# Layer 0's context in three parts, and other orders at the start of four stages, in a four-layer transformer kernel

## The reference

```
x = x + xattn_L(layernorm(x), ctx);  x = x + ffn_L(layernorm(x))        L = 0..3
L0 xattn: x1 = LN(q_in)*g1+b1; x2 = LN(ctx)*g2+b2; k = x2@Wk+bk; v = x2@Wv+bv
          softmax(q k^T / 16) v @ Wo + bo          (one head of 256, per batch)
L0 ffn:   8-way router, top 2; silu(x@w0.T+b0)*c0 + silu(x@w1.T+b1)*c1
L1 xattn: 8 heads of 128 over all tokens and all context rows
L1 ffn:   rows rounded to 8 bits, weights to -1/0/1 times mean(|w|); silu(gate)*up, down
L2, L3 xattn: 16 heads of 64, per batch;  L2, L3 ffn: 8 experts, top 2
```

## Time and profile before

| | |
|---|---|
| median of 3 runs (lowest to highest) | 1838.39 us (1838.14 to 1839.67) |
| profiled execution: its time, its span | 1833.6 us, 1831.8 us |
| TensorE, weight load busy | 1727.3 us (94%), 1528.6 us (83%) |
| VectorE, ScalarE, GpSimd busy | 1390.8 us (76%), 1037.4 us (57%), 636.6 us (35%) |
| TensorE's granted clock, mean | 0.986 of 2.4 GHz |
| stages begin at (us of the span) | 0, 105.9, 136.3, 945.7, 1005.2, about 1357, 1410.7, 1721.9 |

### The profile page before, as it was taken

One profiled execution on the slowest core, in us unless ns is written; L12 is line 12 of the kernel. 1 busy time (PEld: TensorE's weight loads), 2 busy tenths in 40 slices (PEclk: granted clock), 3 DMA queues, 4 the chain that ended last, 5 costly groups with the idle time before them and its releaser, 6 DMA issues. The chain is left out here.

```text
span 1831.8 us, 31026 instructions
## 1 busy us (share of the span) xinstructions
PE 1727.3 (94%) x11308; PEld 1528.6 (83%) x11311; DVE 1390.8 (76%) x3101; ACT 1037.4 (57%) x2291; POOL 636.6 (35%) x904
## 2 busy tenths in 40 slices
PE   6979999999999999999978899999979999999799
PEld 6657898999989998989875788888857888888698
DVE  6568787877778787878767677777777788888775
ACT  3355656555655655554655566666650677777542
POOL 0613030210203030302100465656661467666542
PEclk9999999999999999999999999999989999999899
DMA  5011000000000000000020111111000000000111
GB/s 177 34 54 38 1 24 1 1 24 1 24 1 24 1 24 1 16 1 1 1 92 7 67 62 55 61 56 61 10 1 18 9 16 17 17 10 4 31 54 42
DMA packets 19480, 52.19 MB, mean 28 GB/s; under 512 B 2809, under 2 KB 7554, under 8 KB 17666
## 3 DMA queue, kind: packets, MB, share of 16 engines
q1 hardware_dynamic: 18466, 49.39, 8.1%
q10 hardware_dynamic: 864, 0.83, 0.1%
HBM read 49.29 MB, written 0.92 MB: 27 GB/s over the span
## 5 line engine op out<-in xcount | busy, mean ns | idle before, releaser
L1476 ACT ACTIVATE a_pH<-banks 125x512 fp32r<-125x512 f32 (+1 forms) x384 | 203.5, 544 | 268.3 <-PE banks L221 193.8
L1573 DVE TENSOR_TENSOR a_pL<-banks,a_pH 125x512 fp32r<-125x512 f32 (+1 forms) x384 | 235.9, 623 | 107.1 <-ACT a_pH L1476 105.1
L2160 POOL TENSOR_TENSOR a_prob<-a_prob,a_rinv 112x750 f32<-112x750 f32 x128 | 184.0, 1437 | 190.2 <-DVE a_rinv L2484 189.7
L1537 DVE TENSOR_SCALAR_CACHE_REDUCE a_prob<-banks 128x500 f32<-128x500 f32 x336 | 221.5, 677 | 4.8 <-PE banks L221 3.9
L1312 POOL TENSOR_TENSOR a_head_oH<-a_o,ones 128x256 fp32r<-128x256 f32 (+1 forms) x23 | 15.6, 678 | 579.5 <-DVE a_o L1581 579.5
L1358 PE MATMUL banks<-ident,a_prob 128*125 128x128 f32 x1344 | 201.3, 274 | 4.5 <-ACT a_prob L1455 2.3
L1455 ACT ACTIVATE a_prob<-a_prob,a_nmax 128x1000 f32<-128x1000 f32 x168 | 187.9, 1121 | 30.7 <-DVE a_nmax L1540 30.7
L221 PE MATMUL banks<-a_pH,a_head_vH 125*128 125x256 f32 (+1 forms) x576 | 199.8, 347 | 5.2 <-DVE a_pL L1573 4.2
L1358 PEld LDWEIGHTS banks<-ident,a_prob 128*125 128x125 f32 x1344 | 186.3, 188 | 7.5 <-DVE a_head_qL L1171 3.5
L221 PE MATMUL banks<-a_pH,a_head_vL 125*128 125x256 f32 (+1 forms) x576 | 173.2, 301 | 0.0
L221 PE MATMUL banks<-a_pL,a_head_vH 125*128 125x256 f32 (+1 forms) x576 | 172.4, 299 | 0.0
(11 more groups left out here) (401 smaller groups left out, 4870.6 us busy)
## 6 DMA issues: line engine op xcount, KB each, us to landing
a_w_out<-in_f_out SPq DMA_DIRECT2D x6, 1024.0 KB, 4.8
a_w_in<-in_f_in SPq DMA_DIRECT2D x12, 512.0 KB, 4.7
f_raw<-in_f_w SPq DMA_DIRECT2D x9, 513.0 KB, 3.6
pair_raw<-in_a_qk SPq DMA_DIRECT2D x16, 256.0 KB, 2.6
pair_raw<-in_a_w SPq DMA_DIRECT2D x8, 384.0 KB, 3.0
combined<-in_f_w SPq DMA_DIRECT2D x12, 256.0 KB, 3.0
a_v<-in_ctx_rows SPq DMA_DIRECT2D x4, 576.0 KB, 7.5
a_kT<-in_f_w SPq DMA_DIRECT2D x2, 1024.0 KB, 5.7
```

What stands on the lines that cost most here:

```text
L1476: act.activation(pH[:, c % RING, 0:wide], TB[c % 4][0:KB, 0:wide], ACT.Copy).then_inc(t_high, 1)
L1537: dve.tensor_scalar(prob[:, at, c * CHUNK:(c + 1) * CHUNK], SB[c % 3][:, 0:CHUNK], SCALE, None, ALU.mult, ALU.max, accum_out=chunk_max[:, ...
L1573: dve.tensor_tensor(pL[:, c % RING, 0:wide], TB[c % 4][0:KB, 0:wide], pH[:, c % RING, 0:wide].bitcast(F32), ALU.subtract).then_inc(t_done, 1)
L2160: pool.tensor_tensor(both, both, rinv[:, n % RING, :].unsqueeze(2).to_broadcast([SEQ, 2, KEYS]), ALU.mult).then_inc(p_normed, 1)
```

## The change

In layer 0's attention the context is loaded, taken statistics of, rooted and normed in three parts of 8 tiles, with semaphores for each; `part_stats(n)` waits for its part and stands between `lows` of the part before. ScalarE scales and copies the weights in one operation per half (`scale=g2`) straight behind its first sqrt, and VectorE cuts each half with one scalar_tensor_tensor. On TensorE and ScalarE a chunk's keys are followed by its two value units; x is turned behind value 8, the queries come behind keys 5. The three sums of absolute values move, with their loads and the mean, from the end of this stage into layer 0's FFN, between its Silus. There `KEYS_AHEAD` is 2 and a chunk more stands behind tile 2. In layer 1's FFN the Silu table is loaded first and the scaling stands behind three key copies, not five. In the 64-wide attentions `queries(0, 1)` moves from the first step to behind the second scores, the values behind them shift (with `NEXT` = 3 in layer 2 and 1 in layer 3), and VectorE cuts all but one of the first value units before the turned x.

```diff
-        LOADS = 4
+        LOADS = PARTS                     # 3
@@ layer0_attention, vector
-            layer_norm_stats(dve, ln_c, qc, ctx_rows, KTILES, ready=lambda i: (ctx_loaded[i // PER], 16))
-            layer_norm_roots(dve, ln_c, qc)
-            normed(0)
-            normed(1)
-
+            part_stats(0)
+            layer_norm_roots(dve, ln_part[0], qc[0])
+            normed(0)
             dve.wait_ge(kv_bias_filled, 1)
             dve.tensor_tensor(kv_bias[:], B[7][:, 0:2 * KT], bkv, ALU.add).then_inc(kv_bias_ready, 1)
+            normed(1)
             for j in range(2):
-                dve.tensor_scalar(wkv[:, :, j, :], wkv[:, :, j, :], g2[:, j:j + 1], None, ALU.mult).then_inc(w_scaled, 1)
-            normed(2)
-            lows(0)
-            dve.wait_ge(w_high, 1)
-            dve.tensor_tensor(wkvL[:], wkv[:], wkvH[:].bitcast(F32), ALU.subtract).then_inc(w_cut, 1)
-            for g in range(1, NG):
-                if g + 2 < NG:
-                    normed(g + 2)
-                lows(g)
+                dve.wait_ge(w_high, j + 1)
+                dve.scalar_tensor_tensor(wkvL[:, :, j, :], wkv[:, :, j, :], g2[:, j:j + 1], wkvH[:, :, j, :].bitcast(F32),
+                                         ALU.mult, ALU.subtract).then_inc(w_cut, 1)
+            lows(0)
+            part_stats(1)
+            layer_norm_roots(dve, ln_part[1], qc[1])
+            normed(2)
+            lows(1)
+            normed(3)
+            part_stats(2)
+            layer_norm_roots(dve, ln_part[2], qc[2])
+            normed(4)
+            lows(2)
+            normed(5)
+            lows(3)
             dve.wait_ge(x_loaded, 16)
             layer_norm_twice(dve, ln_x, qx, s.x, xa)
+            lows(4)
+            lows(5)
@@ layer0_attention, scalar: the new order
+            layer_norm_scalar(act, ln_part[0], qc[0])
+            act.wait_ge(wkv_loaded, 32)
+            for j in range(2):
+                act.activation(wkvH[:, :, j, :], wkv[:, :, j, :], ACT.Copy, scale=g2[:, j:j + 1]).then_inc(w_high, 1)
+            highs(0)
+            layer_norm_scalar(act, ln_part[1], qc[1])
+            highs(1)
...
+            highs(2)
+            layer_norm_scalar(act, ln_part[2], qc[2])
+            keys(1)
...
+            keys(2)
+            layer_norm_scalar(act, ln_x, qx, 1)
+            values(4)
+            layer_norm_scalar(act, ln_x, qx, 2)
+            values(5)
+            highs(4)
...
+            values(9)
+            keys(5)
+            values(10)
+            exps(0)
+            values(11)
             exps(1)
@@ layer0_attention, tensor: the new order
+            for c in range(3):
+                keys(c)
+                values(2 * c)
+                values(2 * c + 1)
+                turn_context(c + 2)
+            keys(3)
+            turn_context(5)
+            values(6)
+            values(7)
+            keys(4)
+            values(8)
+            pe.wait_ge(c_cut, 2 * NG)
+            turn_x()
+            values(9)
+            keys(5)
+            queries()
+            values(10)
@@ layer0_ffn
-        KEYS_AHEAD = 3
-        KEYS_BEHIND = (3, 4, 5)
+        KEYS_AHEAD = 2
+        KEYS_BEHIND = (2, 3, 4, 5)
...
+            for m in range(SUMS):
+                sp.dma_start(quant_raw[:, m, :], dram["f1_w"][:, m, :]).then_inc(quant_loaded[m], 16)
...
                 act.activation(post[:, i % POST, :], EB[i % 4][:, :], ACT.Silu).then_inc(post_ready, 1)
+                if i < SUMS:
+                    act.wait_ge(quant_loaded[i], 16)
+                    act.activation(quant_raw[:, i, :], quant_raw[:, i, :], ACT.Abs, accum_out=abs_sum[:, i:i + 1]).then_inc(abs_summed, 1)
                 if i in KEYS_BEHIND:
                     key_high(KEYS_AHEAD + KEYS_BEHIND.index(i))
@@ layer1_ffn, scalar (KEYS_FIRST = 3)
-            for c in range(CHUNKS - 1):
+            load_table(act, s, ACT.Silu)
+            for c in range(KEYS_FIRST):
                 key_high(c)
-            load_table(act, s, ACT.Silu)
             act.wait_ge(x_step, 4)
             for i in range(TILES):
                 act.activation(big[:, i, :], xn[:, i, :], ACT.Copy, scale=scale[:, i:i + 1], bias=MAGIC).then_inc(x_scaled, 1)
-            key_high(CHUNKS - 1)
+            for c in range(KEYS_FIRST, CHUNKS):
+                key_high(c)
@@ attention_heads64, tensor (NEXT = AHEAD_VALUES)
             queries(0, 0)
-            values(0, AHEAD_VALUES)
+            values(0, NEXT)
             pe.wait_ge(ql.done, GROUPS)
             scores(0, 0)
-            for u in range(AHEAD_VALUES + 1, 5):
+            for u in (NEXT + 1, NEXT + 2):
                 values(0, u)
             scores(0, 1)
-            values(0, 5)
+            queries(0, 1)
             turn(0)
-            for u in (6, 7):
-                values(0, u)
+            values(0, NEXT + 3)
             scores(0, 2)
-            for u in (8, 9):
+            for u in LAST_VALUES:
                 values(0, u)
@@ attention_heads64, vector
+            EARLY = max(VALUES_BEFORE - 1, 0)
+            for u in range(EARLY):
+                values(0, u)
             turn_vector(dve, ql, LNB, s.xnTH, s.xnTL)
```

More of the change, by code:

```diff
@@ L276, in layer0_attention @@
         ln_x = s.ln
-        qc = layer_norm_semaphores(sem, "a0_lc")
+        qc = [layer_norm_semaphores(sem, f"a0_lc{n}") for n in range(PARTS)]
         qx = layer_norm_semaphores(sem, "a0_lx")
+        ln_part = []
+        for n in range(PARTS):
+            part, tiles = Names(), slice(n * (KTILES // PARTS), (n + 1) * (KTILES // PARTS))
+            part.stats, part.mean_var, part.root = ln_c.stats[:, tiles, :], ln_c.mean_var[:, tiles, :], ln_c.root[:, :, tiles]
+            ln_part.append(part)
         g1, b1 = cols[:, 0:2], cols[:, 2:4]
@@ L584, in scores, with keys, values @@
                     for k in range(KT)]).then_inc(s_filled, 1)
-            pe.wait_ge(kv_bias_ready, 1)
-            for n in range(KTILES // 2):
-                if n == TURN_AT:
-                    turn_x()
-                if n == QUERIES_AT:
-                    queries()
-                if n == SCORES_AT:
-                    for b in range(AHEAD):
-                        scores(b)
+            def keys(c):
+                cols = slice(c * CHUNK, (c + 1) * CHUNK)
+                pe.wait_ge(c_cut, 2 * c + 2)
+                for e in range(KT):
+                    n, at = KT * c + e, slice(e * P, (e + 1) * P)
+                    need(pe, k_done, n - 1)
+                    split_products(pe, B[4 + n % 2][:, 0:CHUNK], [
+                        (wkvH[:, 0, 0, at], cH[:, cols]), (wkvH[:, 0, 0, at], cL[:, cols]), (wkvL[:, 0, 0, at], cH[:, cols]),
+                        (wkvH[:, 0, 1, at], cT[:, cols]), (wkvL[:, 0, 1, at], cT[:, cols])]).then_inc(k_filled, 1)
+            def values(n):
                 need(pe, v_done, n - 1)
@@ L601, in _ @@
                 last.then_inc(v_filled, 1)
+            pe.wait_ge(kv_bias_ready, 1)
+            for c in range(3):
[3 more added lines that the diff above has]
+                turn_context(c + 2)
+            keys(3)
+            turn_context(5)
+            values(6)
+            values(7)
+            keys(4)
+            values(8)
+            pe.wait_ge(c_cut, 2 * NG)
[4 more added lines that the diff above has]
+            values(10)
+            for b in range(AHEAD):
+                scores(b)
+            values(11)
             def turn(b):
@@ L640, in _ @@
                 output_tile(i)
-            pe.wait_ge(abs_summed, 3)
-            pe.matmul(B[4][:, 0:3], s.ones[:], abs_sum[:], start=True, stop=True).then_inc(abs_total, 1)
 def router_buffers(sb, tag):
@@ L912, in _ @@
                     keys(KEYS_AHEAD + KEYS_BEHIND.index(i))
+                if i == TILES - 2:
+                    pe.wait_ge(abs_summed, SUMS)
+                    pe.wait_ge(q.shifted, 1)
+                    pe.matmul(B[3][:, 0:SUMS], s.ones[:], abs_sum[:], start=True, stop=True).then_inc(abs_total, 1)
 Q_W, K_W = (0, 1), (2, 3)
@@ L2007, in attention_heads64 @@
         count("v", (0, u))
+    NEXT = AHEAD_VALUES
+    LAST_VALUES = [u for u in range(NEXT + 4, UNITS) if u not in FIRST_VALUES_AT]
     count("q", (0, 0))
-    for u in range(AHEAD_VALUES, UNITS):
-        if u not in FIRST_VALUES_AT:
-            count("v", (0, u))
+    for u in range(NEXT, NEXT + 3):
+        count("v", (0, u))
+    count("q", (0, 1))
+    count("v", (0, NEXT + 3))
+    for u in LAST_VALUES:
+        count("v", (0, u))
     for h in range(HEADS):
```

115 lines of the change are left out of this document (44 added, 71 removed).

## The result

| | before | after |
|---|---|---|
| median of 6 runs (lowest to highest) | 1838.54 us (1837.86 to 1840.28) | 1826.69 us (1824.47 to 1828.05) |
| ratio after / before, 95% interval | | 0.9933 (0.992 to 0.9946) |
| profiled execution, its span | 1833.6 us, 1831.8 us | 1826.62 us, 1824.8 us |
| TensorE's granted clock, mean | 0.986 | 0.985 |

The change took 11.85 us off the median (9.9 to 14.7 by the interval); 9.1 were forecast, and 1829.3 for the time. TensorE's busy time is 1727.3 us in both profiles; the gain is idle time that went.

The account below looks back on a forecast made before the run. TensorE is busy for 94% of the span, so time could come only from its idling or waits between engines. Terms 2.1 + 2.2 - 1.1 + 1.9 + 4.2 - 0.2 = 9.1 took 1838.4 to 1829.3 us, range 1825.0 to 1834.5.

Parts of the forecast that it names:

- start of layer 0's attention: Context in three parts gives TensorE work while VectorE norms; queries 2.1 us earlier, ends 1.0 and 3.0.
- sums out of its end: End of layer 0's attention: without the three sums VectorE, not ScalarE, is last; 2.2 us saved, ends 1.8 and 2.3.
- layer 0's FFN: Sums between ScalarE's Silus delay the Silu and key copy VectorE wants; 1.1 us lost, ends 0.5 gained and 3.0 lost.
- layer 1's FFN: Table load moves into ScalarE's idle time, scaling waits behind three key copies; 1.9 us saved, ends 1.0 and 2.2.
- layer 2's attention, to the fifth scores: Queries start earlier and the fifth scores wait for the exps alone; 4.2 us saved, ends 2.5 and 5.0.
- layer 3's attention: Values 5 to 9 stand behind the third scores, delaying the fourth; 0.2 us lost, ends 1.0 gained and 1.0 lost.
- I count nothing for it: Layer 0's attention: GpSimd waits for x's norm and so starts 7.5 us earlier; priced at nothing.
- Rival C: Layer 0's FFN: sums between Silus need a table each, six loads of 1.28, 7.7 us more, 1837; chance 0.08.
- with an idle of 1.0 I expect none of it: Layer 2's attention, first queries: with the wait cut from 2.59 us, TensorE's clock would not fall to 1.2 GHz.
- rival A: Layer 2's attention: earlier starts wait longer at the fifth scores, 4.2 becomes 0 to 1, 1833; chance 0.15.
- D: Layer 0's attention: TensorE never reaches 2.4 GHz while context parts arrive, 1848; chance 0.05 together with other mishaps.
- B: Start of layer 0's attention gives nothing, VectorE being the bound with three roots in its way, 1831.4; chance 0.10.

Follow-up runs that it names:

- e3: Kernel before with only the new start order of layer 0's attention, the three sums still at that stage's end; 1834.75 us, ratio 0.9986.
- e6: Changed kernel plus transposes nobody reads on TensorE at the end of layer 1's FFN, before layer 2's attention; 1825.97 us, ratio 0.993.
- e7: Changed kernel with three key chunks, as before, ahead of the turned x in layer 0's FFN; 1829.11 us, ratio 0.9949.
- e9: Changed kernel plus unread transposes at the ends of seven stages and ahead of layer 3's FFN's turns; 1828.37 us, ratio 0.9952.
- e10: As e9, plus 20 unread transposes ahead of the fifth scores in the 64-wide attentions; 1824.78 us, ratio 0.9933.
- e4: Changed kernel with the old order of the two 64-wide attentions; 1829.98 us, ratio 0.9959.
- e1: Kernel before, unedited, in one more profiled execution; 1838.98 us, span 1837.2 us.
- e5: Changed kernel with GpSimd's split of the raw context held back until ScalarE writes the first turned x; 1826.91 us, ratio 0.9944.
- e12: Changed kernel with GpSimd's split of the raw context started behind VectorE's fourth low, not behind x's norm; 1837.74 us, ratio 0.9998.
- e8: Changed kernel with the old layer 1 FFN and 16 unread transposes ahead of its first turn; 1831.63 us, ratio 0.9963.
- e2: Kernel before with only the new order of the two 64-wide attentions; 1834.53 us, ratio 0.9986.
- e11: Changed kernel with the fills of e6 and the 20 unread transposes ahead of the fifth scores; 1823.22 us, ratio 0.992.

## Why the prediction was right, term by term

| term | forecast | measured | from |
|---|---|---|---|
| start of layer 0's attention | +2.1 | +2.9 | e3 against three old profiles |
| sums out of its end | +2.2 | +2.3 | e3 against after |
| layer 0's FFN | -1.1 | about -0.9 | means of 4 old (31.1) and 7 new (32.0; e6 among them, without e7, e9, e10) |
| layer 1's FFN | +1.9 | +3.4 | 59.5 to 56.1, steady |
| layer 2's attention, to the fifth scores | +4.2 | +3.6 | 29.25 to 25.66, full clock at the start |
| the same, whole stage | +4.2 | +1.4 on the mean, +3.25 at much the same clock | 4 old, 6 new profiles; e4 against after |
| layer 3's attention | -0.2 | about -0.4 on the mean, -0.75 and -1.85 at like starts | means 310.5 and 310.85; below |

The sum of the measured stages is 8.7, and 0.6 comes from layer 1's attention, whose code is the same: 9.3 with 9.1 forecast. That these two agree is partly luck: layer 2 brought 2.8 less than forecast on the mean, layer 1's FFN 1.5 and layer 0's start 0.8 more. The timed 11.85 is above both, and its interval begins at 9.9. The timed executions show where most of the rest lies. At the same mean clock the two kernels are 8.7 and 9.6 apart (at 0.985 the medians are 1835.35 and 1826.62, at 0.984 they are 1836.20 and 1826.63, from two or three executions each), but the kernel before is mostly at 0.980 to 0.982 and the changed kernel at 0.983 to 0.985. So some 9 us come at the same mean clock, about what the sum says, and 2 to 3 go with a clock that the sum did not have. Against e1, the usual execution of the kernel before, the changed kernel's profile is 12.4 shorter, and its stages are so by 5.2, 0.5, 0.2, 3.5, 2.4, 0.2, 0.8 and -0.3. How much of the higher clock the change itself brought is shown in one place only: the stretch inside layer 1's FFN, in all five profiles of its old order and in those of its new one only in e9 and e10.

*Start of layer 0.* The total was right to 0.8 by two errors of opposite sign. The first is that a transfer's size was changed and the landing of what comes beside it was not moved: with 8 tiles a load the weights, brought by ScalarE's queue, came 0.94 later (no run changes the loads alone, so the cause is taken from the order of events). That took the queries from 54.0 to 54.9. The second stands in the forecast as "I count nothing for it": GpSimd starts 6.2 us earlier, its split of the context is over sooner, and the batch loop is 1.8 shorter. e5 gives 0.8 of it back, and e12 shows that where the two engines meet can cost several times that. Smaller slips: the three parts have two more roots than one part, not four, and 2.3 + 1.2 + 1.5 + 1.2 + 2.3 is 8.5, not 8.4.

*Layer 0's end and its FFN.* The steps came as written, the wait of 1.0 for the key copy included (0.94), except that VectorE's updates of x start 1.6 earlier in the stage and not 1.1: the stage's first products ran at full clock (0.46 for the 0.71 of the earlier trace rows), the 0.4 that was not counted. So in this pair of profiles the stage is only 0.4 longer; the 0.9 is a mean over profiles that scatter from 30.8 to 33.5. Rival C is out, no table is loaded between sum and Silu.

*Layer 1's FFN.* The step mis-sized is "The rest of the stage is a chain through VectorE and follows". ScalarE's turned copies came 2.0 earlier, as forecast, but VectorE's first product of the halves 3.36 (13.56 into the stage for 16.92). In the old order TensorE waits twice there, 1.92 and 1.53, and is at half clock for 3.4 us behind the second in every profile. In the new order the first wait is gone, one of 1.92 stands in the second's place, and the clock stays at 1.00 behind it, except in e9 and e10, which price such a stretch there at 1.1 to 1.3. Why it stays is open: e8 filled the old order's first wait and the clock fell all the same.

*Layer 2.* The reckoning by steps was right to 0.7 in the six profiles with a full clock at the start (fifth scores at 25.65 to 25.69 for 25.03). What failed is "with an idle of 1.0 I expect none of it": I looked at the clock behind the wait that the change removes and not ahead of the stage, nor behind the wait of 2.3 us that it creates at the fifth scores. There rival A was right in its wording (what starts earlier waits longer at the fifth scores), and the clock is the price of that wait. On the mean the stage is nearer to A's 0 to 1 than to my 4.2. The forecast's own sign of being wrong, fifth scores less than 3 us nearer to the stage's start, is there in the changed kernel's profile: 28.39 for 29.25, 0.9 nearer, with the start at half clock.

*Layer 3.* The fourth scores wait for the late value units, as forecast, but the cost is above the 0.2. Where both orders start the stage at half clock the fifth scores come 31.1 into it (e2, e8) for 30.35, and the stage takes 311.9 for 311.16. Where both start at full clock they come at 28.4 (the changed kernel and others) for 27.65 (e4), and it takes 310.3 for 308.47, with 3.4 us at half clock behind the wait of 1.45. So the new order loses in layer 3; the second of these comparisons rests on a single profile of the old order.

*From profile to runs.* I added 4.8 to the profiled time as if it belonged to the kernel. It belonged to that execution (e1): the changed kernel's profiled time equals its median. Profile against profile the change is worth 7.0, below the forecast, runs against runs 11.85, above it.

*The range.* Its low ends are mis-added. 1.0 + 1.8 - 3.0 + 1.0 + 2.5 - 1.0 is 2.3 and not 3.8, which would put that end at 1836.1; the high ends do make 14.0. The time lies well inside either way.

D and B did not come: VectorE was the bound as B said, but TensorE had its work beside it, and its clock stood at 2.4 GHz from 17.7 on.

## What to carry to other kernels

Price a reordering at the step where the next wait ends last, then ask what the new wait does to TensorE's clock: here 3.6 us of earlier work bought 1.4 on the mean, and twenty transposes that nobody reads, in the new wait of 2.3 us, another 3.2 (e6 to e11, 350.50 to 347.26); in layer 3, where they outlast the wait, they cost 0.6. Fills pay where TensorE sets the pace behind them; at the ends of stages they raised the clock and not the speed (e9). An engine "off the path" that shares something with the one on it is a term of the sum: one wait on GpSimd, moved by 8.5 us, cost 11 us (e12). And ask at which mean clock the profile of before was taken: here it was the best case of its kernel, by 5 us.

## What was not expected of the hardware

The places of half clock differ between executions of one program: 24.8 and 35.1 us summed, spans 1831.8 and 1837.2, with the same idle time (2.15) ahead of a stage that started at full clock once and at half the other time. VectorE's tensor_scalar of 128x256 floats takes 0.34 us alone and 0.96 beside GpSimd's casts and subtractions, while its statistics of seven such tiles take 2.39 beside them and 2.38 alone (e12, and the changed kernel).
